# Gate and up of two token blocks as seven block products instead of eight, with their sums made by VectorE and GpSimd

## The reference

```
x = x + stencil(x)          # Laplacian along tokens and channels, plus zR * y * (1 - y)
x = x + attention_pool(x)   # tanh(x @ W1 + b1) @ v as scores, masked softmax, weighted sum / count
x = x + fc(x)               # gelu(x @ fc1.T + b) @ fc2.T, 192 shared and 64 columns of a chosen expert
x = x + experts(x)
```

```
g = einsum('bsd,edf->ebsf', h, Wg);  u = einsum('bsd,edf->ebsf', h, Wu)
expert_outs = einsum('ebsf,efd->ebsd', silu(g) * u, Wd)
expert_output = einsum('be,ebsd->bsd', gating_probs, expert_outs)
shared = einsum('bsf,fd->bsd', silu(h @ Sg) * (h @ Su), Sd)
return (1.0 - sg) * expert_output + sg * shared
```

## Time and profile before

| what | value |
|---|---|
| median of 3 runs | 1377.25 us |
| span of the profiled execution | 1373.0 us |
| TensorE busy | 1346.5 us, 98% of the span |
| VectorE busy | 755.6 us, 55% |
| ScalarE busy | 329.8 us, 24% |
| GpSimd busy | 45.7 us, 3% |
| mean granted TensorE clock | 0.992 |

### The profile page before, as it was taken

How to read it: one execution, slowest core, us unless ns; L and a number is a source line. 1 busy time by engine, 2 the same in 40 slices (tenths; PEclk the granted TensorE clock), 3 DMA queues, 4 the chain that set the end, 5 groups by cost and what they waited for, 6 DMA issues and landing times.

```text
span 1373.0 us, 16497 instructions
## 1 busy us (share of the span) xinstructions
PE 1346.5 (98%) x5832; PEld 1079.9 (79%) x5832; DVE 755.6 (55%) x1231; ACT 329.8 (24%) x565; POOL 45.7 (3%) x48
## 2 busy tenths in 40 slices
PE   6799999999999999999999999999999999999998
PEld 4568888888888888888888888888888888888886
DVE  6956555555555555555555555555555555554444
ACT  2555622211112222111122221121222211111111
POOL 7500000000000000000000000000000000000000
PEclk8899999999999999999999999999999999999999
DMA  8020200000000000000000000000000000000000
GB/s 249 15 92 9 84 23 23 23 23 23 23 23 23 23 23 23 23 23 23 23 23 23 23 23 23 23 23 23 23 23 23 23 23 0 0 0 1 26 19 15
DMA packets 16432, 39.59 MB, mean 29 GB/s; under 512 B 6562, under 2 KB 9122, under 8 KB 16290
## 3 DMA queue, kind: packets, MB, share of 16 engines
q1 hardware_dynamic: 15536, 39.39, 8.8%
q10 hardware_dynamic: 882, 0.02, 0.0%
HBM read 37.31 MB, written 2.10 MB: 29 GB/s over the span
## 4 chain that ended last, share of the span: by engine, by line
PE 96%; DVE 3%; DMA 1%; ACT 0%; issue 0%; SPq 0%; DVEq 0%; ACTq 0%
PE ps L858 96%; DMA xT<-in_x_rows 1%; DVE x_dn L683 0%; DVE w_lo L713 0%; DVE gate L570 0%; DVE xT L609 0%; DVE poly L602 0%; DVE row_max L644 0%; DVE xT L729 0%; PE ps L875 0%; DVE denom L664 0%; DVE x_lo L721 0%; DVE x_dn L658 0%; DVE nb_all L595 0%; DVEq L45 0%
## 5 line engine op out<-in xcount | busy, mean ns | idle before, releaser
L858 PE MATMUL ps<-x_hi,w_hi 128*128 (+1 forms) x1216 | 480.7, 395 | 2.8 <-DVE x_lo L721 2.7
L858 PE MATMUL ps<-x_lo,w_hi 128*128 (+1 forms) x1216 | 480.7, 395 | 0.0
L858 PE MATMUL ps<-x_hi,w_lo 128*128 (+1 forms) x1216 | 477.4, 393 | 0.0
L828 DVE SCALAR_TENSOR_TENSOR hidden<-stage,gate,ps 128x512 f32<-128x512 f32 x288 | 215.3, 748 | 440.6 <-ACT stage L516 440.6
L516 ACT ACTIVATE stage<-ps 128x512 f32<-128x512 f32 x288 | 172.2, 598 | 928.3 <-PE ps L858 928.2
L858 PEld LDWEIGHTS ps<-x_hi,w_hi 128*128 128x128 f32 x1216 | 228.1, 188 | 60.1 <-issue 2.9
L858 PEld LDWEIGHTS ps<-x_hi,w_lo 128*128 128x128 f32 x1216 | 228.5, 188 | 54.3
L858 PEld LDWEIGHTS ps<-x_lo,w_hi 128*128 128x128 f32 x1216 | 228.2, 188 | 52.1
L858 PE MATMUL ps<-h_hi,w_hi 128*128 128x512 f32 x640 | 252.3, 394 | 0.0
L858 PE MATMUL ps<-h_lo,w_hi 128*128 128x512 f32 x640 | 251.9, 394 | 0.0
L858 PE MATMUL ps<-h_hi,w_lo 128*128 128x512 f32 x640 | 251.2, 392 | 0.0
(11 more groups left out here) (105 smaller groups left out, 286.2 us busy)
## 6 DMA issues: line engine op xcount, KB each, us to landing
raw<-in_moe_w SPq DMA_DIRECT2D x36, 768.0 KB, 4.3
out_x<-xT SPq DMA_DIRECT2D x8, 256.0 KB, 2.4
xT<-in_x_rows SPq DMA_DIRECT2D x2, 528.0 KB, 4.8
x_up<-in_x_rows SPq DMA_DIRECT2D x2, 520.0 KB, 6.6
...
```

What stands on the lines that cost most here:

```text
L828: nc.vector.scalar_tensor_tensor(hidden[:, k % PAIR, :], stage[:, k % PAIR, :], gate[:, ds(e, 1), ds(tb, 1)].rearrange("p e t -> p (e t)") ...
L858: return nc.tensor.matmul(out_ap, lhsT, rhs, start=first, stop=last)
```

## The change

In the expert stage the outer order is the same (9 experts), but the unit is a group: one chunk k of the hidden width for a pair of token blocks (a round; 2 rounds, so 16 groups for each expert). Gate (A11, A12 for the two channel chunks) and up (A21, A22) are the rows of a 2 x 2 block matrix, and the two token blocks (B11, B21 and B12, B22) its other operand. Their product needs 8 block products; it is now made from 7 with sums of blocks on both sides:

- weight sums per chunk: S1 = A21 + A22, S2 = S1 - A11, S3 = A11 - A21, S4 = A12 - S2
- token sums per round: T1 = B12 - B11, T2 = B22 - T1, T3 = B22 - B12, T4 = B21 - T2
- products: P1 = A11 B11, P5 = S1 T1, P6 = S2 T2, P7 = S3 T3, and A12 B21, S4 B22, A22 T4

TensorE adds what it can in PSUM (A12 B21 on P1, S4 B22 on P5, P7 and A22 T4 on P6). The other sums need P1 and P5 twice, so ScalarE copies both out of PSUM (p1_out, p5_out), GpSimd adds the copies (p15_sum), and VectorE adds from PSUM (p6_sum, gate1_sum, up1_sum and the first half of hidden0_mul). VectorE then multiplies silu and up for each token block (hidden0_mul, hidden1_mul) without the gating factor; the factor moves to the addition of the outputs (outputs_added). The high halves of the hidden products move from VectorE to ScalarE (hidden0_high, hidden1_high). Down products stay as they are.

The weights come as one piece for each expert and chunk: 6 tiles of 128x128 by one DMA into a ring of four places, in which VectorE adds the four sums (piece_sums); ScalarE makes the high half of 9 tiles in one instruction (piece_high) and VectorE the low half (piece_low). There is one set of 8 high and low pieces rather than two slots; a piece is overwritten when the last down product of its chunk is done. The token blocks and sums are split once into 7 high and 7 low tiles for each round. Tiles of the early stages share their place in SBUF with those of the expert stage. The host puts the weights in the order of the pieces. The old expert_block and expert of each engine, the second weight slot, x3_high and x3_low are gone; in the fc stage the early pieces and the tokens of round 0 take their place. The core of the diff (the removed functions stand above):

```diff
+        RAWS, RT, WT, XT = 4, 10, 9, 7
...
+        piece = place("piece", RAW, [P, RAWS, RT, P])
...
+        A21, A11, A12, A22, D0, D1, S1, S2, S3, S4 = range(RT)
+        B11, B21, B22, T4, T1, T2, T3 = range(XT)
+        ROUNDS = 2
+        GROUPS = ROUNDS * FC
...
+            def piece_load(e, k):
+                src = moe_w[e, k, :, :] if isinstance(e, int) else \
+                    moe_w[ds(e, 1), k, :, :].rearrange("e p w -> (e p) w")
+                sp.dma_start(piece[:, k % RAWS, 0:S1, :], src.rearrange("p (t m) -> p t m", m=P)) \
+                  .then_inc(piece_in[k % RAWS], 16)
...
+            def p15_sum(e, i):
+                n = e * GROUPS + i
+                pool.wait_ge(p1_copied, n + 1)
+                pool.wait_ge(p5_copied, n + 1)
+                nc.gpsimd.tensor_tensor(p5_copy[:, :], p5_copy[:, :], p1_copy[:, i % 2, :],
+                                        ALU.add).then_inc(p15_summed, 1)
+            with pool.Fori(0, E) as e:
...
+                    p15_sum(e, i)
 
...
+            def piece_high(e, k, after_round=True):
+                q = e * FC + k
+                act.wait_ge(wsum_done, 4 * q + 4)
+                if after_round:
+                    act.wait_ge(down0_done, (e - 1) * GROUPS + FC + k + 1)
+                nc.scalar.activation(w_hi[k][:, :, :], piece[:, k % RAWS, A11:RT, :], ACT.Copy).then_inc(whi_done, 1)
...
+            def p1_out(e, i):
+                n = e * GROUPS + i
+                act.wait_ge(p1_ps, n + 1)
+                if not starts(e, i, 2):
+                    act.wait_ge(hidden0_done, n - 1)
+                nc.scalar.activation(p1_copy[:, i % 2, :], ps[:, BANK_A, :], ACT.Copy).then_inc(p1_copied, 1)
...
+            def p5_out(e, i):
...
+                nc.scalar.activation(p5_copy[:, :], ps[:, BANK_E, :], ACT.Copy).then_inc(p5_copied, 1)
+            def gate0(e, i):
...
+                nc.scalar.activation(silu0[:, i % 2, :], ps[:, BANK_A, :], ACT.Silu).then_inc(silu0_done, 1)
+            def gate1(e, i):
...
+                nc.scalar.activation(silu1[:, :], g1_sum[:, :], ACT.Silu).then_inc(silu1_done, 1)
+            def hidden0_high(e, i):
...
+                nc.scalar.activation(h0_hi[:, i % 2, :], hidden0[:, :], ACT.Copy).then_inc(h0_hi_done, 1)
+            def hidden1_high(e, i):
...
+                nc.scalar.activation(h1_hi[:, :], hidden1[:, :], ACT.Copy).then_inc(h1_hi_done, 1)
...
+            def expert(e, first, last):
+                for i in range(GROUPS):
+                    before = not starts(e, i, 1)
+                    p1_out(e, i)
+                    if before:
+                        hidden1_high(*earlier(e, i, 1))
+                    p5_out(e, i)
+                    gate0(e, i)
+                    if before:
+                        hidden0_high(*earlier(e, i, 1))
+                    gate1(e, i)
+                    if first and i < FC:
...
+                        piece_high(e, i + 4)
+                    elif i >= FC + 2 and not last:
+                        piece_high(e + 1, i - FC - 2)
+            expert(0, True, False)
+            with act.Fori(1, E - 1) as e:
...
+            def piece_sums(e, k):
+                w = [piece[:, k % RAWS, t, :] for t in range(RT)]
+                dve.wait_ge(piece_in[k % RAWS], (e * (FC // RAWS) + k // RAWS + 1) * 16)
+                done = 4 * (e * FC + k)
+                nc.vector.tensor_tensor(w[S1], w[A21], w[A22], ALU.add).then_inc(wsum_done, 1)
+                nc.vector.tensor_tensor(w[S3], w[A11], w[A21], ALU.subtract).then_inc(wsum_done, 1)
+                dve.wait_ge(wsum_done, done + 1)
+                nc.vector.tensor_tensor(w[S2], w[S1], w[A11], ALU.subtract).then_inc(wsum_done, 1)
+                dve.wait_ge(wsum_done, done + 3)
+                nc.vector.tensor_tensor(w[S4], w[A12], w[S2], ALU.subtract).then_inc(wsum_done, 1)
+            def piece_low(e, k):
+                dve.wait_ge(whi_done, e * FC + k + 1)
+                nc.vector.tensor_tensor(w_lo[k][:, :, :], piece[:, k % RAWS, A11:RT, :],
+                                        w_hi[k][:, :, :].bitcast(f32), ALU.subtract).then_inc(wlo_done, 1)
...
+            def hidden1_low(e, i):
+                n = e * GROUPS + i
+                dve.wait_ge(h1_hi_done, n + 1)
+                nc.vector.tensor_tensor(h1_lo[:, :], hidden1[:, :], h1_hi[:, :].bitcast(f32),
+                                        ALU.subtract).then_inc(h1_ready, 1)
+            def hidden0_mul(e, i):
+                n = e * GROUPS + i
+                dve.wait_ge(u0_ps, n + 1)
+                nc.vector.tensor_tensor(hidden0[:, :], p1_copy[:, i % 2, :], ps[:, BANK_B + i % 2, :],
+                                        ALU.add).then_inc(u0_done, 1)
+                dve.wait_ge(silu0_done, n + 1)
+                dve.wait_ge(u0_done, n + 1)
+                nc.vector.tensor_tensor(hidden0[:, :], silu0[:, i % 2, :], hidden0[:, :],
+                                        ALU.mult).then_inc(hidden0_done, 1)
+            def p6_sum(e, i):
+                n = e * GROUPS + i
+                dve.wait_ge(p6_ps, n + 1)
+                dve.wait_ge(p1_copied, n + 1)
+                if not starts(e, i, 1):
+                    dve.wait_ge(silu1_done, n)
+                nc.vector.tensor_tensor(g1_sum[:, :], ps[:, BANK_B + i % 2, :], p1_copy[:, i % 2, :],
+                                        ALU.add).then_inc(p6_summed, 1)
+            def gate1_sum(e, i):
+                n = e * GROUPS + i
+                dve.wait_ge(g1_ps, n + 1)
+                dve.wait_ge(p6_summed, n + 1)
+                nc.vector.tensor_tensor(g1_sum[:, :], ps[:, BANK_E, :], g1_sum[:, :], ALU.add).then_inc(g1_summed, 1)
+            def hidden0_low(e, i):
...
+                nc.vector.tensor_tensor(h0_lo[:, i % 2, :], hidden0[:, :], h0_hi[:, i % 2, :].bitcast(f32),
+                                        ALU.subtract).then_inc(h0_ready, 1)
+            def up1_sum(e, i):
+                n = e * GROUPS + i
+                dve.wait_ge(p7_ps, n + 1)
+                dve.wait_ge(p15_summed, n + 1)
+                nc.vector.tensor_tensor(u_sum[:, :], ps[:, BANK_B + i % 2, :], p5_copy[:, :],
+                                        ALU.add).then_inc(u1_done, 1)
...
+            def hidden1_mul(e, i):
+                n = e * GROUPS + i
+                dve.wait_ge(silu1_done, n + 1)
+                dve.wait_ge(u1_done, n + 1)
+                nc.vector.tensor_tensor(hidden1[:, :], silu1[:, :], u_sum[:, :], ALU.mult).then_inc(hidden1_done, 1)
+            def outputs_added(e, r, h):
+                done = (down0_done, down1_done)[h]
+                dve.wait_ge(done, (e * ROUNDS + r + 1) * FC)
                 for c in range(DC):
-                    xs = xT[:, c, ds(tb * TB, TB)]
-                    nc.vector.tensor_tensor(xs, xs, ps[:, OUT + c, :], ALU.add).then_inc(out_free, 1)
...
+            def expert(e, first, last):
+                for i in range(GROUPS):
+                    before = not starts(e, i, 1)
+                    if before:
+                        hidden1_low(*earlier(e, i, 1))
+                        hidden0_mul(*earlier(e, i, 1))
+                    p6_sum(e, i)
+                    if before:
+                        hidden0_low(*earlier(e, i, 1))
...
+                    elif 2 <= i <= 4:
+                        if i < 4:
+                            piece_sums(e, i + 4)
+                        piece_low(e, i + 3)
+                    elif i >= FC + 2 and not last:
+                        piece_sums(e + 1, i - FC - 2)
+                        if i > FC + 2:
+                            piece_low(e + 1, i - FC - 3)
+                    gate1_sum(e, i)
+                    up1_sum(e, i)
+                    hidden1_mul(e, i)
+            expert(0, True, False)
...
+            def product(bank, k, w, p, x, first, last):
+                return split_mm(ps[:, bank, :], ((w_hi[k][:, w - 1, :], w_lo[k][:, w - 1, :]),
+                                                 (xc_hi[p][x][:, :], xc_lo[p][x][:, :])), first, last, True)
...
+            def down(e, i, h, c):
...
+                if k == 0 and not starts(e, i, FC):
+                    pe.wait_ge(acc_read, (e * ROUNDS + p - 1) * NT + DC * (1 - h) + c + 1)
+                if c == 0:
+                    pe.wait_ge((h0_ready, h1_ready)[h], e * GROUPS + i + 1)
+                high, low = ((h0_hi[:, i % 2, :], h0_lo[:, i % 2, :]), (h1_hi[:, :], h1_lo[:, :]))[h]
+                last = split_mm(ps[:, ACC + DC * h + c, :], ((w_hi[k][:, D0 - 1 + c, :], w_lo[k][:, D0 - 1 + c, :]),
+                                                             (high, low)), k == 0, k == FC - 1, True)
+                if c == DC - 1:
+                    last.then_inc((down0_done, down1_done)[h], 1)
+            def up0_end(e, i):
+                pe.wait_ge(u1_done, e * GROUPS + i + 1)
+                product(BANK_B + i % 2, i % FC, A22, i // FC, T4, False, True).then_inc(u0_ps, 1)
```

(30 more changed lines are left out.)

518 lines of the change are left out of this document (301 added, 217 removed).

## The result

The changed kernel takes 1387.8 us in the median (1386.0 to 1391.6), the kernel before 1376.4 (1373.7 to 1381.0) on the same chip: a ratio of 1.0086 [1.0061, 1.0111], 11.8 us slower by the ratio. Forecast were 1407 us and +30. The direction is as forecast, the size is not: the cost is 40% of it.

What follows compares the result with a forecast made beforehand. The order of hand-overs between VectorE and ScalarE, not TensorE, was to bound the changed kernel: span 1373 + 28 (expert stage) + 2 (fc stage) = 1403, median 1407 us, 2.2% slower, own range 1388 to 1432.

Steps and rivals of the forecast that it cites:

- TensorE's count and the new bound: Expert stage: 432 matmuls less, 5400 in the profile, TensorE busy near 90%; the order of VectorE's and ScalarE's operations decides.
- 33 matmuls, 7.65 us: TensorE's work in one expert-stage group: 33 matmuls at 0.2317 us, 7.65 us instead of 8.34 for 36.
- piece_high's term: On ScalarE ahead of p1_out and hidden1_high: hidden1_low comes 2.29 us after hidden1_mul instead of 1.39, +0.90.
- The port: GpSimd and VectorE operations with two SBUF inputs exclude each other: hidden0_mul's product ends 0.40 us late, 35 us in all.
- The piece work in the chain: piece_sums add 0.95 us and piece_low 1.27 to VectorE's chain; with a piece_high before, a group takes 9.61.
- The fc stage, +2: Ahead of the experts, VectorE's and ScalarE's load grows in the last two fc blocks: nothing to 3 us, taken as 2.
- First and last expert: The first expert takes 141.2 us, the last 127.6, plus 3.1 for the last group's uncovered chain.
- the step from the profiled span to the median: 4.25 us added to any span worked out, from a profiled span of 1373.0 and a median of 1377.25.
- The table: Timetable of one group from gate1_sum in VectorE's order: 6.49 us plus additions for piece work and outputs; group 8 at 7.83.
- Rival 1: TensorE still bounds the expert stage, waiting being covered: median 1282 us, half covered about 1345; chance 0.16.
- Rival 2: The port between GpSimd and VectorE costs nothing in the expert stage: 1372 us; chance 0.10.
- Rival 3: Long hand-overs, ScalarE's table load in the chain, or TensorE's clock falling: 1440 us and more; chance 0.08.

Runs made afterwards that it cites:

- b_placed: The kernel before with its five largest tiles (xT, x_hi, raw, first weight slot) moved behind the small ones: 1348.5 us, 0.9803 of the kernel before.
- a_split544: The changed kernel with its later tiles (tokens, hidden tiles, pieces 0 to 4) moved by 544 bytes: 1396.4 us, 1.0157 of the kernel before.
- a_high_early: The changed kernel with piece_high moved on ScalarE to directly behind gate0 of the next group: 1348.5 us, 0.9815 of the kernel before.
- a_small_pieces: The changed kernel with piece sums and halves of experts 1 to 8 made for 8 columns instead of 128: 1272.2 us, 0.9249 of the kernel before.
- a_high_split_spread: The changed kernel with piece_high behind gate0, GpSimd's sum as two halves and the piece sums spread over other groups: 1348.4 us, 0.9808 of the kernel before.
- a_both_gated: The changed kernel with piece_high behind gate0, hidden0_mul's add ahead of hidden1_low, GpSimd's sum held until hidden0_mul's product is done: 1324.8 us, 0.9631 of the kernel before.
- a_small_p15: The changed kernel with GpSimd's sum made for 8 of 512 tokens: 1354.9 us, 0.9865 of the kernel before.

## Why the prediction was right in direction and off in size

1. TensorE's count and the new bound: right. 5400 matmuls, 92% busy, chain on VectorE and ScalarE.
2. "33 matmuls, 7.65 us": mis-sized, the first of the two terms that failed. I took 0.2317 us as the cost of a matmul at full rate; it was the cost at that placement of tiles. It is 0.2267 after, a light group 7.48. On the kernel before, the better placement is worth 27 us (b_placed), on the changed one 8 to 10 (a_split544), since its piece groups wait for the chain, not for TensorE. On equal placement the change costs 0.9803 against 1.0086, about 39 us, not 12. That the measured cost is as small as 12 us is therefore luck: the new layout gave back what I had not counted.
3. piece_high's term, +0.90 in the group behind it: mis-sized, +0.67, the second term that failed. The step behind it is "on ScalarE 0.60 apart for 0.63": that pair had waited for VectorE. ScalarE's distance between starts is about 0.1 less than the length, not 0.03, in three places in this wait: silu to piece_high 0.53 (so that it starts 0.13 ahead of hidden1_mul and not 0.06), piece_high to p1_out 1.06, p1_out to hidden1_high 0.47. Together 0.23. With the small terms an expert came to 135.0 instead of 136.8: -1.3 in the six piece groups, -0.2 and -0.1 in groups 4 and 0, which also have a piece_high before them, -0.5 in the light ones by matmul distance, +0.35 in group 8. The mechanism of the piece_high term, piece_high in the way of the chain, is shown (a_high_early).
4. The port: right. Forecast 0.40 a group and 35 us in all, measured 0.35 and 30. That a sum from PSUM goes free is right too: the add at 703.05 takes 0.68 with GpSimd's sum beside it all the time. By the rule of the Trainium skill (GPSIMD Engine Reference, section 1 Specifications) contention comes with VectorE instructions of two SBUF inputs; the trace agrees with 1.04 us against 0.69 and an unchanged 0.68.
5. The piece work in the chain: right. Piece groups 9.39 against 9.61, and without that work 7.0 to 7.5 (a_small_pieces).
6. The fc stage, +2: not settled. The experts start at 165.55 us in this profile, 1.2 earlier than before, but in the profiles of the other kernels with the same early stages and placement they start between 164.9 (a_high_split_spread) and 170.7 us (a_both_gated). One profile of each kernel doesn't give the sign.
7. First and last expert: 140.4 against 141.2, and 129.6 with the tail against 130.7.

In sum the profiled span is 1385.3 against 1403: 14.4 in the expert stage, 3.2 before it. The rest of the 19 us is the step from the profiled span to the median: 2.5 here, where I took 4.25. The 14.4 are -11.6 in the groups behind a piece_high (seven middle experts, 1.66 each), -3.7 in their light groups, +2.5 in group 8, and -1.9 in the first and the last expert, all rounded. So of the ratio's error (1.0216 forecast, 1.0086 measured, 17.9 us) some 12 us are the wait behind piece_high, by ScalarE's distance between starts, 8 to 10 are the matmul's distance, and group 8 takes 2.5 back. The order of hand-overs that I forecast was the right mechanism.

The table lacked what lengthens group 8: with TensorE not ahead, p1_out waits for its product, and hidden1_high stands behind p1_out in ScalarE's order, so hidden1_low comes 1.71 after hidden1_mul instead of 1.39:

```profile
774.37 0.69 DVE L1046 TENSOR_TENSOR hidden<-silu,u_sum 128x512 f32<-128x512 f32 x1
...
774.93 0.60 ACT L612 ACTIVATE p_copy<-ps 128x512 f32<-128x512 f32 x1 [0.68 <-PE ps L1108]
775.42 0.62 ACT L647 ACTIVATE h_hi<-hidden 128x512 fp32r<-128x512 f32 x1
...
776.08 0.69 DVE L1001 TENSOR_TENSOR h_lo<-hidden,h_hi 128x512 fp32r<-128x512 f32 x1 [1.02 <-ACT h_hi L647]
```

Rival 1 needed the chain of a piece group under 8.0: it was 9.4; with the reorderings and the gated sum it is 8.46, and then the kernel is faster than the one before (0.9631, and 0.9803 of that is placement). Rival 2 is refuted by a_small_p15. Rival 3 had three parts. Of ScalarE's table loads, 16 before in the expert stage, one is left; hand-overs were as forecast but for the 0.78 of the add; and the clock did not fall, in a stretch of the changed kernel that answers to the earlier trace rows:

```profile
480.00:800.00 320.00, 299.98 (x1274) 235.44 (x1273) 263.14 (x414) 149.25 (x249) 49.23 (x38) 1.00 0.07 21
```

TensorE pauses twice in each piece group there, 0.8 and 0.55 us, and is busy 94%, and the clock stays at 1.00.
